# Attention scores from two float32r halves in two half-height row tiles of the array, instead of three bf16 parts over its full height

## What is computed

```python
N_HEAD = 16                                   # hs = 256 / 16 = 16
k_eff = (W_dq.T @ W_uq.T @ W_uk).reshape(nh, hs, n_kvl)
v_eff = jnp.transpose((W_uv.T @ W_o.T).reshape(n_kvl, nh, hs), (1, 0, 2))
c_kv = x @ W_dkv.T
q = (x @ W_dq.T @ W_uq.T).reshape(B, T, nh, hs)
q_lat = jnp.einsum('bqhd,hdl->bhql', q, k_eff)
attn = jnp.einsum('bhql,bkl->bhqk', q_lat, c_kv) / sqrt(hs)
attn = jax.nn.softmax(jnp.where(causal[None, None], attn, -jnp.inf), axis=-1)
y_lat = jnp.einsum('bhqk,bkl->bhql', attn, c_kv)
y = jnp.einsum('bhql,hld->bqhd', y_lat, v_eff)
```

## Time and profile before

| what | value |
|---|---|
| median of 3 runs | 1451.26 us |
| the profiled execution | 1452.64 us |
| its span, first to last instruction | 1450.8 us |
| PE / PEld / DVE / ACT / POOL busy | 1218.1 / 755.3 / 880.1 / 610.2 / 447.5 us |
| attention's two passes, about | 60 to 645 us of the span |
| mean granted TensorE clock | 0.92 of full speed |

### The profile page before, as it was taken

How to read it: one execution, slowest core, us unless ns; L and a number is a source line. 1 busy time by engine, 2 the same in 40 slices (tenths; PEclk the granted TensorE clock), 3 DMA queues, 4 the chain that set the end, 5 groups by cost and what they waited for, 6 DMA issues and landing times. The chain is left out here.

```text
span 1450.8 us, 32359 instructions
## 1 busy us (share of the span) xinstructions
PE 1218.1 (84%) x13530; PEld 755.3 (52%) x13530; DVE 880.1 (61%) x1900; ACT 610.2 (42%) x1207; POOL 447.5 (31%) x663
## 2 busy tenths in 40 slices
PE   3779999999999999989999346566987858699993
PEld 1434444444444444337888323245665647488882
DVE  4466767676788777715434755677867362354346
ACT  1426666666666766655222322122332212142222
POOL 2420505142200000014231556443663313342304
PEclk7889999999999999999999768778999979899996
DMA  5492535344455333000000000011111100000003
GB/s 153 131 148 90 89 45 89 56 78 67 73 63 62 49 45 45 2 1 1 1 0 1 17 17 10 21 32 29 33 29 32 35 25 12 2 1 0 1 1 116
DMA packets 78754, 61.66 MB, mean 43 GB/s; under 512 B 41360, under 2 KB 65552, under 8 KB 78480
## 3 DMA queue, kind: packets, MB, share of 16 engines
q1 hardware_dynamic: 77456, 57.18, 21.9%
q10 hardware_dynamic: 1152, 2.41, 0.5%
HBM read 38.20 MB, written 20.97 MB: 41 GB/s over the span
## 5 line engine op out<-in xcount | busy, mean ns | idle before, releaser
L694 ACT ACTIVATE weights<-psum 128x512 f32<-128x512 f32 (+1 forms) x608 | 322.4, 585 | 159.4 <-PE psum L607 157.5
L739 DVE TENSOR_REDUCE maxima<-psum 128x1 f32<-128x512 f32 (+3 forms) x432 | 262.2, 662 | 57.4 <-PE psum L538 56.3
L607 PE MATMUL psum<-q_stack,k_stack 99*128 99x512 bf16 (+3 forms) x768 | 223.7, 328 | 1.3 <-ACT weights L694 1.1
L538 PE MATMUL psum<-k_stack,q_stack 96*128 96x512 bf16 (+3 forms) x768 | 213.0, 328 | 5.8 <-DMA k_stack<-qk_parts 4.1
L624 PE MATMUL psum<-weights,v_rows 128*17 128x512 f32 (+3 forms) x1536 | 162.0, 494 | 0.1
L510 POOL TENSOR_TENSOR residual<-residual,att_o 128x256 f32<-128x256 f32 x32 | 23.2, 725 | 364.0 <-DVE att_o L772 364.0
L900 PE MATMUL psum<-f_xT,f_weights_hi 128*128 128x512 f32 x384 | 123.5, 403 | 0.0
L739 DVE TENSOR_REDUCE negmax<-psum 128x1 f32<-128x384 f32 (+3 forms) x176 | 102.3, 634 | 27.8 <-PE psum L538 26.2
L607 PEld LDWEIGHTS psum<-q_stack,k_stack 99*128 99x128 bf16 x768 | 72.5, 98 | 83.1 <-ACT weights L694 38.6
L965 ACT ACTIVATE f_gates<-psum,ffn_biases 128x512 f32<-128x512 f32 x72 | 49.7, 690 | 155.8 <-PE psum L906 155.8
L1335 PE MATMUL psum<-d_w_qkb,d_hT 128*128 128x260 f32 x128 | 48.0, 510 | 68.3 <-DVE d_attnT_k_kb_v L1505 57.8
(11 more groups left out here) (165 smaller groups left out, 2277.9 us busy)
## 6 DMA issues: line engine op xcount, KB each, us to landing
qk_parts<-a_parts SPq DMA_DIRECT2D x32, 384.0 KB, 3.6
q_stack<-qk_parts SPq DMA_DIRECT2D x90, 128.0 KB, 7.1
k_stack<-qk_parts SPq DMA_DIRECT2D x90, 128.0 KB, 7.8
residual<-in_x SPq DMA_DIRECT2D x8, 512.0 KB, 7.5
out_x<-residual SPq DMA_DIRECT2D x8, 512.0 KB, 3.8
ffn_weights<-in_ffn_w ACTq DMA_DIRECT2D x1, 2048.0 KB, 9.1
systems<-d_a_rows SPq DMA_DIRECT2D x32, 64.0 KB, 1.8
d_systems<-systems SPq DMA_DIRECT2D x4, 512.0 KB, 4.8
```

Source lines behind the costliest of these rows:

```text
L538: m = e.matmul(out[:, i * width:(i + 1) * width], self.qst[st][0:self.ROWS, h, qb * P:(qb + 1) * P], self.kst[st][0:self.ROWS, h, k0:k0 + ...
L607: m = e.matmul(out[:, j * width:(j + 1) * width], self.kst[st][0:self.ROWS + self.MAX_ROWS, h, kb * P:(kb + 1) * P], self.qst[st][0:self.R ...
L694: e.activation(self.weights[n % 2][:, heads[0]:heads[-1] + 1, 0:width], bank[self.score_bank[n, i]][:, 0:len(heads) * width].rearrange("p ...
L739: e.tensor_reduce(to, bank[self.bank[item]][:, 0:len(heads) * width].rearrange("p (h x) -> p h x", h=len(heads)), AXIS_X, ALU.max, negate= ...
```

## The change

q and k are now split into two float32r parts each (a 12-bit high half and the rest), of which three products are kept, so a head's stack is 3 x 16 = 48 rows, and with two rows for the maximum 50. A stack holds two heads one above the other: in a pair of heads `a`, the even one (`j` = 0) on rows 0 to 49, the odd one (`j` = 1) on rows 64 to 113. Their matmuls therefore carry the tile size 64 x 128 and the row position 0 or 64. The masks stay bf16 matmuls over all 128 rows. Score groups now go to bank pairs (0, 1) and (2, 3), the even head in the first bank and the odd one in the second, with one mask for each bank and one exponential over both; 20 groups a unit where there were 38. A `max` item is still one bank, now of one parity of heads (one head, or two of the same parity): 40 a unit. The ring of the other banks is 4, 5, 6. A unit's stacks are loaded by 12 DMAs as before, of the same size, now with float32 elements; a `qk` item is written as 512 KB instead of 384 KB; the maxima go out by four DMAs instead of three. The split itself takes ACT and DVE in the prologue, and two POOL operations later.

```diff
-    SPLIT = ((0, 1, 0, 1, 2, 0), (0, 0, 1, 1, 0, 2))
-    PRODUCTS, ROWS, MAX_ROWS = 6, 6 * HS, 3
+    SPLIT = ((0, 0, 1), (0, 1, 0))
+    PRODUCTS, ROWS, MAX_ROWS, HALF = 3, 3 * HS, 2, P // 2
-    PROLOGUE_BANKS, SCORE_BANKS, RING = (0, 1, 2, 3, 4, 5, 6), (0, 1, 2), (3, 4, 5, 6)
+    PROLOGUE_BANKS, RING = (0, 1, 2, 3, 4, 5, 6), (4, 5, 6)
...
-            self.qst = [sb(f"q_stack{i}", [P, HPU, T], BF16) for i in range(STACKS)]
-            self.kst = [sb(f"k_stack{i}", [P, HPU, T], BF16) for i in range(STACKS)]
+            self.qst = [sb(f"q_stack{i}", [P, 2, T], F32R) for i in range(STACKS)]
+            self.kst = [sb(f"k_stack{i}", [P, 2, T], F32R) for i in range(STACKS)]
...
-                n = min(HPU, BANK // width)
-                self.pairs += [(qb, c, width, range(h, h + n)) for h in range(0, HPU, n)]
+                n = min(2, BANK // width)
+                self.pairs += [(qb, c, width, j, range(a, a + n)) for a in range(0, 2, n) for j in range(2)]
...
-        self.scored = [[range(h, h + n) for h in range(0, HPU, n)]
-                       for n in [min(HPU, BANK // self.span(n)[1]) for n in range(len(self.steps))]]
+        self.scored = [[range(a, a + n) for a in range(0, 2, n)]
+                       for n in [min(2, BANK // self.span(n)[1]) for n in range(len(self.steps))]]
...
-                self.score_bank[n, i] = self.SCORE_BANKS[at % 3]
+                self.score_bank[n, i] = at % 2
...
@@ def gpsimd
-            if item[0] == "qk":
+            if item[0] == "qk" and item[1] >= self.EARLY:
...
                 e.tensor_copy(parts[:, 0, :], raw[:, :]).then_inc(*s["raw_hi"].did(i))
...
+                e.tensor_tensor(parts[:, 1, :], raw[:, :], parts[:, 0, :], ALU.subtract).then_inc(*s["lo"].did(i))
...
@@ def tensor, a max item
+                st, k0, rows = u % STACKS, c * BANK, slice(j * self.HALF, j * self.HALF + self.ROWS)
...
-                for i, h in enumerate(heads):
-                    m = e.matmul(out[:, i * width:(i + 1) * width], self.qst[st][0:self.ROWS, h, qb * P:(qb + 1) * P],
-                                 self.kst[st][0:self.ROWS, h, k0:k0 + width], start=not diagonal and i == 0, stop=True,
+                for i, a in enumerate(heads):
+                    m = e.matmul(out[:, i * width:(i + 1) * width], self.qst[st][rows, a, qb * P:(qb + 1) * P],
+                                 self.kst[st][rows, a, k0:k0 + width], start=not diagonal and i == 0, stop=True,
...
@@ def scores
-            if self.diagonal(n):
-                e.matmul(out[:, 0:len(heads) * width].rearrange("p (h x) -> p h x", h=len(heads))[:, :, 0:P], k.mask16[:, :],
...
+            for j in range(2 if self.diagonal(n) else 0):
+                e.matmul(bank[2 * pair + j][:, 0:len(heads) * width].rearrange("p (a x) -> p a x", a=len(heads))[:, :, 0:P],
...
-            for j, h in enumerate(heads):
-                m = e.matmul(out[:, j * width:(j + 1) * width],
-                             self.kst[st][0:self.ROWS + self.MAX_ROWS, h, kb * P:(kb + 1) * P],
-                             self.qst[st][0:self.ROWS + self.MAX_ROWS, h, q0:q0 + width],
+            for at, a in enumerate(heads):
+                for j in range(2):
+                    rows = slice(j * self.HALF, j * self.HALF + self.ROWS + self.MAX_ROWS)
+                    m = e.matmul(bank[2 * pair + j][:, at * width:(at + 1) * width], self.kst[st][rows, a, kb * P:(kb + 1) * P],
+                                 self.qst[st][rows, a, q0:q0 + width],
...
@@ def exps
-            e.activation(self.weights[n % 2][:, heads[0]:heads[-1] + 1, 0:width],
-                         bank[self.score_bank[n, i]][:, 0:len(heads) * width].rearrange("p (h x) -> p h x", h=len(heads)),
+            e.activation(self.weights[n % 2][:, 2 * heads[0]:2 * heads[-1] + 2, 0:width].rearrange("p (a j) x -> p j a x", j=2),
+                         k.psum_pairs[pair][:, :, 0:len(heads) * width].rearrange("p j (a x) -> p j a x", a=len(heads)),
```

More of the change, by code:

```diff
@@ L387, in release @@
         if kind == "qk":
-            return s["rest" if a[0] < self.EARLY else "raw"](self.part(*a))
-        return s[{"turn": "xT_out", "lat": "lat_out", "v": "v_out", "max": "max_red", "negmax": "max_rest", "out": "att_o"}[kind]](*a)
+            return s["early_lo" if a[0] < self.EARLY else "raw"](self.part(*a))
+        return s[{"turn": "xT_out", "lat": "lat_out", "v": "v_out", "max": "max_red", "negmax": "max_lo", "out": "att_o"}[kind]](*a)
     def part(self, g, which, mt):
@@ L516, in stacked @@
         def stacked(u, half):
-            return s[f"stack_in{u % STACKS}"](u, half if u == 0 else 1, self.PRODUCTS - 1, 1)
+            return s[f"stack_in{u % STACKS}"](u, half if u == 0 else 1, self.PRODUCTS - 1, 1, 1)
         def make(item):
@@ L674, in copy_out @@
                 if a[0] >= self.EARLY:
-                    for w in unmet(s["lo"](i - 2)):
+                    for w in unmet(s["lo"](i - 1) if i - 1 >= self.part(self.EARLY, 0, 0) else None):
                         e.wait_ge(*w)
-                    e.activation(self.rest[i % 2][:, :], out[:, :], ACT.Copy).then_inc(*s["raw"].did(i))
+                    e.activation(self.rest[:, :], out[:, :], ACT.Copy).then_inc(*s["raw"].did(i))
                     return
                 e.activation(self.parts[i % 4][:, 0, :], out[:, :], ACT.Copy).then_inc(*s["hi"].did(i))
-                for w in unmet(s["rest"](i)):
-                    e.wait_ge(*w)
-                e.activation(self.parts[i % 4][:, 1, :], self.rest[i % 2][:, :], ACT.Copy).then_inc(*s["mid"].did(i))
             if kind == "v":
@@ L727, in take @@
                 out = bank[self.bank[item]]
[L728 removed]
+                for w in unmet(s["hi"](i)):
                     e.wait_ge(*w)
[L730 to L731 removed]
+                e.tensor_tensor(self.parts[i % 4][:, 1, :], out[:, :], self.parts[i % 4][:, 0, :], ALU.subtract
+                                ).then_inc(*s["early_lo"].did(i))
             if kind == "max":
                 u, w_at = a
[L734 removed]
+                qb, c, width, j, heads = self.pairs[w_at]
                 n, hs_ = u % 2, slice(heads[0], heads[-1] + 1)
[L736 removed]
+                to = self.maxima[n][:, j, hs_, qb - QB // 2, c] if qb >= QB // 2 else self.negmax[n][:, j, hs_, qb]
                 for w in unmet(s["max_mm"](u, w_at), s["negmax_T"](u - 2) if u >= 2 else None):
                     e.wait_ge(*w)
[L739 removed]
+                e.tensor_reduce(to, bank[self.bank[item]][:, 0:len(heads) * width].rearrange("p (a x) -> p a x", a=len(heads)),
                                 AXIS_X, ALU.max, negate=True).then_inc(*s["max_red"].did(u, w_at))
@@ L776, in vector @@
         for st in range(STACKS):
-            e.memset(self.kst[st][self.ROWS:self.ROWS + self.MAX_ROWS, :, :], 1.0).then_inc(*s["k_ones"].did(st))
+            for j in range(2):
+                e.memset(self.kst[st][j * self.HALF + 32:(j + 1) * self.HALF, :, :].bitcast(F32), 1.0).then_inc(*s["k_ones"].did(st))
         e.memset(bank[7][:, :], 0.0).then_inc(*s["o_zero"].did())
```

105 lines of the change are left out of this document (43 added, 62 removed).

## The result

Four runs of the changed kernel took 1625.45 to 1648.37 us, median **1634.75**; four of the kernel before beside them 1448.43 to 1452.02, median 1450.16. The ratio is 1.128 [1.118, 1.138]: slower, and slower than forecast. The profiled execution took 1626.1 us, 174 more than the one before.

The account below looks back on a forecast made before the run. PE was taken to bound attention at full clock; -4.4 + 6.6 + 4.1 + 0.5 = +6.8 us a unit, times 13.85 = +94, on 1452.6 gives 1547 us, range 1462 to 1610.

Parts of the forecast that it names:

- rival 4: Score and maximum matmuls on PE: the two halves don't overlap, +12.3 us a unit, 1623 us; chance 5%.
- What bounds the kernel now: Steady attention, 120 to 590 us: PE bounds, busy 467.7 of 470.0 us at granted clock 1.00; 13.85 units of 33.9 us.
- Changes of shape: PE, between full-height masks and half-height matmuls: 90 changes a unit instead of 24, 0.10 us each, 6.6 us lost.
- Loads behind a change and short matmuls: PE: 41 exposed float32r loads at 0.10 us lose 4.1 us a unit; 16 matmuls of 128 columns lose 0.5.
- Rows side by side: Scores and maxima on PE: two heads overlap in two row tiles, 15.8 to 11.4 us, gain 4.4 us a unit.
- rivals 3 and 4: Rival 3: the two halves' loads queue behind each other on PE, +10.9 us a unit, 1604 us; chance 12%.
- Other engines nothing: ACT, DVE, POOL, DMAs and bank rings: all cost nothing while PE is the bound.
- Three items take PE over 2 us: Ring one bank shorter: a bank must be free three items later, over 2 us of PE against 0.68 for a reduction.
- Rival 2: PE's changes of shape: only the drain is paid, the load is hidden, +2.7 us a unit, 1490 us; chance 13%.
- rival 1: PE: a change between full and half height is free, -3.9 us a unit, 1398 us; chance 15%.
- the forecast's own case: PE's order in attention: drains and loads behind changes both paid, +6.8 us a unit, 1547 us; chance 55%.
- wrong altogether: Sign against the forecast: PE waiting for banks, with DVE's reductions as releaser, or the granted clock leaving 1.00.

Follow-up runs that it names:

- experiment 11: The changed kernel with stacks read as bf16 upper halves and both heads' matmuls in the upper half of the rows, so pairs run one after the other: 1824.3 us.
- experiment 5: The changed kernel with its half-height matmuls reading the upper 16 bits of each float32r value as bf16: 1500.3 us.
- experiment 2: The kernel before with mask matmuls cut to rows 0 to 63, adding 80 changes of tile shape a unit: 1582.7 us.
- experiment 10: The changed kernel with every mask matmul made four times, 24,576 more full-height columns a unit: 1721.6 us.
- experiment 4: The changed kernel with both heads of a pair taken from the upper row tile, same 90 changes of shape, no overlap: 2011.7 us.
- experiment 7: The changed kernel with scores at full height (both heads added) and maxima one at a time in their head's half: 1625.3 us.
- experiment 1: The changed kernel with masks also in half height, each two matmuls of 64 columns in its head's row tile: 1468.8 us, ratio 1.013.

## Why the prediction was wrong

The direction held, and so did the price of a change and of a load in PE's order. The time came out 79 us over the forecast in the profiled execution, and outside the range. It lies nearest to rival 4's 1623 us, which the starts of the pairs refute: the number alone would have named the wrong cause.

**The step that failed** is in "What bounds the kernel now": "at a granted clock of 1.00", carried over to the changed kernel. Every term of the sum was priced at full clock. From 150 to 820 us the clock was 0.88, so 2 x 0.12 x 670 = 161 us ran at 1.2 GHz. What a unit loses there: experiment 11's late unit takes 64.1 us at 0.52, almost all at 1.2 GHz, and at full clock it would be about 39 (34.5 of experiment 5, plus the 4.5 by which the two differ in a unit that both ran at full clock, 285.3 to 328.8 against 238.1 to 277.1 us). That is a factor of about 1.7, not 2, and an estimate. Of the 161 us, 161 x (1 - 1/1.7) = **66 us** were lost to the clock.

**The terms at full clock** add up to about 14 us more than forecast:

- *Changes of shape*, 66 x 0.10 = 6.6: right, 0.10 by experiment 2.
- *Loads behind a change and short matmuls*, 4.1 + 0.5: the change against experiment 5 is 4.4 us in an early unit, which both ran at full clock (43.9, from 159.6 to 203.5 us, against 39.5). Right.
- *Rows side by side*, gain 4.4: the halves start 3 ns apart, so rivals 3 and 4 are out. But the overlap is worth 4.5 us (11 against 5), where 12,032 columns saved at 0.235 per 512 would be 5.5: the gain was about 3.4.
- *Other engines nothing*: off by a little. PE waited for banks of the ring once a unit:

```profile
PE psum L534 <- DVE maxima L734: 7.2, 13, 0.6
```

0.5 us a unit (125 to 740 us). "Three items take PE over 2 us" was wrong where maxima without a mask stand together and overlap: three of them started within 0.29 us (635.72 to 636.01), and the fourth waited 0.55 us for a bank.

So -3.4 + 6.6 + 4.6 + 0.5 = 8.3 us a unit, where the prediction had 6.8; the early unit, all at full clock, grew by 8.6 (43.9 from 35.3). Late units at full clock would be 38.9 (34.5 + 4.4, and again by experiment 10), 7.8 over before. With 7.8 x 13.85 = 108 and the clock's 66 it makes 174 of the 178 us by which attention grew (its end moved from 644 to 822 us); the closeness is partly luck, as each part is known to some us.

**The chances.** Rival 2 (load hidden) is out by experiment 5, rival 1 by experiment 2. Of PE's order the forecast's own case was the right one. The text named the clock as what would make it "wrong altogether", but gave it no chance and no price, and left it out of the range. The rows had a hint: the clock was 0.86 from 60 to 120 us, where PE was idle a quarter of the time.

## What to carry to other kernels

When a change makes matmuls smaller in rows, shorter, or separated by drains and loads, price it twice: at full clock, and again for the share that could fall to 1.2 GHz, which here took about 1.7 times as long. PE's busy share does not warn of it; the row of granted clocks does. Before splitting rows, bring everything around the split to the same tile shape: here masks in half height took 62 of 90 changes away and all but 15 of 185 us of the loss.

## What the runs showed of the hardware

- The granted clock can stand at 0.50 with PE 100% busy (experiment 4, whose scores use 50 of the 128 rows), where it stands at 1.00 with scores on 114 rows (experiment 7). The Trainium skill ("TensorE: Matmul & The Clock Gate", Part 1) has the gate go by how busy the engine has been recently; by the profile's busy share these traces disagree, unless rows that stand idle count as not busy, which fits the runs but was not measured directly.
- More work at the same time: 8,192 further full-height columns a unit changed neither the unit (44.4 and 44.3 us) nor the kernel (1.128 and 1.127), because the clock rose from 0.85 to 0.95.
- At 1.2 GHz a unit of this kind is about 1.7 times as long, not twice (an estimate: 64.1 us at a clock of 0.52 against 39 in experiment 11).
- In one kernel, units of equal work can differ in clock (experiment 1: 0.77 in the unit from 537.0 to 574.3 us, which took 37.3, and 1.00 in the next, which took 30.9), and its runs scatter more (1466.4 to 1484.8) than those of the kernel before (1447.6 to 1457.9). What tips one unit and not the next stays open.
